# Row statistics by accumulating ScalarE passes in a two-part kernel, with another order of first banks, peaks and inputs

## What is computed

```
def _layernorm(x, eps=1e-05):
    m = jnp.mean(x, axis=-1, keepdims=True)
    v = jnp.var(x, axis=-1, keepdims=True)
    return (x - m) / jnp.sqrt(v + eps)

def mx_linear(x, W, b):            # blocks of 32 along the contraction, 8 bits, shared power of two
    return bf16_round(jnp.einsum('btk,ok->bto', mx_quant(x), mx_quant(W)) + b)

def _L0_ffn_ref(inputs, ln_w, ln_b, W1, b1, W2, b2):
    x = residual = bf16_round(inputs)
    h = mx_layernorm(x, ln_w, ln_b)          # mean and variance a second time
    h = mx_gelu(mx_linear(h, W1, b1))        # 1024 -> 4096
    h = mx_linear(h, W2, b2)                 # 4096 -> 1024
    return bf16_round(residual + h)

x = x + jnp.tanh(g_xattn[0]) * _L0_xattn_ref(ctx, ctx, _layernorm(x), ssm_kernel, D, 8)
x = x + jnp.tanh(g_ffn[0]) * _L0_ffn_ref(_layernorm(x), ln_w, ln_b, W1, b1, W2, b2)
```

## Time and profile before

| | |
|---|---|
| median of 3 runs | 1953.61 us (1953.2 to 1955.44) |
| profiled execution | 1954.59 us, its span 1952.8 us |
| PE busy | 1872.4 us, 96% |
| DVE busy | 1640.4 us, 84% |
| ACT busy | 1023.0 us, 52% |
| POOL busy | 881.6 us, 45% |
| mean granted TensorE clock | 0.987 |

### The profile page before, as it was taken

The page is one execution under the profiler, slowest core; times in us unless marked ns, Lnnn a source line. Parts: engine busy times, 40 slices in busy tenths (PEclk is TensorE's granted clock), DMA queues, the critical chain, the costliest instruction groups (busy, mean ns, idle before and its releaser), DMA issues. The chain is left out here.

```text
span 1952.8 us, 28581 instructions
## 1 busy us (share of the span) xinstructions
PE 1872.4 (96%) x11384; PEld 1473.2 (75%) x11432; DVE 1640.4 (84%) x1906; ACT 1023.0 (52%) x1271; POOL 881.6 (45%) x645
## 2 busy tenths in 40 slices
PE   6999999999999989998996997999999999999998
PEld 5888888888888879887885565666677766666773
DVE  5889999988888878888869898989888888889843
ACT  5565555555567767776723453444445544434440
POOL 3888889787888879997960000000000000000000
PEclk9999999999999999999998998999999999999999
DMA  7665657777666667776658421222122211221112
GB/s 243 207 217 170 182 173 223 241 243 256 222 207 186 226 202 230 227 229 207 200 202 300 138 73 53 65 76 77 44 76 77 76 66 55 66 76 55 44 44 76
DMA packets 165478, 294.24 MB, mean 151 GB/s; under 512 B 106145, under 2 KB 106145, under 8 KB 157153
## 3 DMA queue, kind: packets, MB, share of 16 engines
q1 hardware_dynamic: 165344, 292.41, 46.0%
HBM read 222.05 MB, written 45.68 MB: 137 GB/s over the span
## 5 line engine op out<-in xcount | busy, mean ns | idle before, releaser
L373 PE MATMUL y_ps<-kk_hi,slab 128*128 128x352 f32 (+6 forms) x3328 | 892.1, 352 | 33.0 <-DMA slab<-taps_scratch 18.3
L373 PEld LDWEIGHTS y_ps<-kk_hi,slab 128*128 128x128 f32 x3328 | 595.7, 189 | 103.2 <-issue 27.4
L373 PE MATMUL y_ps<-kk_lo,slab 128*128 128x512 f32 (+6 forms) x1664 | 582.0, 350 | 0.0
L1080 PE MATMUL l_ps<-f_xq_T,w_rest 128*128 128x256 bf16 x3136 | 349.2, 274 | 7.4 <-DMA f_xq_T<-f_hq 6.3
L1080 PEld LDWEIGHTS l_ps<-f_xq_T,w_rest 128*128 128x128 bf16 x3136 | 307.6, 98 | 47.6 <-issue 6.7
L373 PEld LDWEIGHTS y_ps<-kk_lo,slab 128*128 128x128 f32 x1664 | 315.1, 189 | 34.7
L861 POOL TENSOR_TENSOR terms<-terms 128x768 f32<-128x768 f32 x127 | 334.3, 2633 | 9.9
L1143 ACT ACTIVATE arena<-l_ps,b_c 128x256 bf16<-128x256 f32 x496 | 206.7, 472 | 248.7 <-PE l_ps L1080 243.4
L1381 POOL TENSOR_TENSOR f_rstd<-f_var_eps,f_neg_half 128x1 f32<-128x1 f32 x28 | 15.3, 548 | 673.0 <-DVE f_var_eps L1201 673.0
L1098 PE MATMUL acc_ps<-raw_room,arena 128*128 128x512 bf16 x993 | 224.6, 379 | 1.6
L1098 PE MATMUL acc_ps<-w_T,arena 128*128 128x512 bf16 x1007 | 222.9, 379 | 0.9
(11 more groups left out here) (148 smaller groups left out, 2295.3 us busy)
## 6 DMA issues: line engine op xcount, KB each, us to landing
slab<-taps_scratch SPq DMA_DIRECT2D x128, 512.0 KB, 4.9
arena<-in_w_m SPq DMA_DIRECT2D x32, 1024.0 KB, 6.8
arena<-x_scratch SPq DMA_DIRECT2D x60, 512.0 KB, 3.8
raw_room<-in_ctx_e SPq DMA_DIRECT2D x64, 384.0 KB, 3.3
arena<-in_w SPq DMA_DIRECT2D x22, 1024.0 KB, 7.5
x_tile<-in_x_t SPq DMA_DIRECT2D x32, 512.0 KB, 4.9
out_t<-arena SPq DMA_DIRECT2D x32, 512.0 KB, 2.6
w_scratch<-arena SPq DMA_DIRECT2D x22, 512.0 KB, 7.3
```

Source lines behind the costliest of these rows:

```text
L373: mm = nc.tensor.matmul(y_ps[:, y_base + begin:y_base + end], slab[s][:, half, d * P:(d + 1) * P], kk_part[s][:, begin - d * PAIR:end - d ...
L1080: mm = nc.tensor.matmul(l1_ps[bank % L1_BANKS][:, a, :], w1_tile(b)[:, k, a * P:(a + 1) * P], inputs[:, k, :], start=(k == 0), stop=(k == ...
```

## The change

Three things move.

1. The row statistics leave DVE. ACT makes them: an Identity pass with scale −1/L whose accumulator is the negated mean, a Square pass with that as its bias whose accumulator is the spread, and a small pass to variance + eps. The passes' main outputs are thrown away: the first pair writes into f_n, the second into the tile's loaded input (spent). SP's next load into that place waits for the second spread (sum2) in place of first_norm (n_ready).
2. first_banks takes bank 4 and 5 of both groups first, then two banks of group 0 to one of group 1, and the rest of group 1 at the end. DVE finishes weight tile 6 at once, and the peaks of group 0 stand behind tiles 8 and 12 (before: 6 and 11).
3. The inputs of groups 3 and 4 (tiles 6 to 9) move: ACT makes tile 4 between the last first banks, tile 5 between the gelus of group 1, tile 6 between banks 3 and 6 of group 2, tile 7 behind group 2's last gelu, and from then on both tiles of a group behind the gelu of a group. DVE weighs tiles 4 and 5 ahead of all peaks of group 1, and tile 7 behind three peaks of group 2. POOL takes each tile's two roots together while g < 4.

The diff, cut to its core:

```diff
-    for b in range(FILL, banks + LAG):
-        first_banks += [(0, b)] if b < banks else []
-        first_banks += [(1, b - LAG)] if b >= FILL + LAG else []
+    first_banks = [(g, b) for g in range(2) for b in range(FILL, KEPT)]
+    for b in range(KEPT, banks):
+        first_banks += [(0, b)]
+        first_banks += [(1, (b + KEPT) // 2)] if (b - KEPT) % 2 == 0 else []
+    first_banks += [(1, b) for b in range(banks) if b >= FILL and (1, b) not in first_banks]
...
-                    sp.wait_ge(n_ready, u - GROUP + 1)
+                    sp.wait_ge(sum2, u - GROUP + 1)
...
         def _(act):
+            def first_statistics(t):
+                i, u = t % GROUP, t - EARLY
+                x = xin[t % X_LOADS]
+                act.wait_ge(x1_loaded[u % X_LOADS], 16 * (u // X_LOADS + 1))
+                if u >= GROUP:
+                    act.wait_ge(hw_ready, u - GROUP + 1)
+                    act.wait_ge(rstd1, u - GROUP + 1)
+                nc.scalar.activation(n_bf[i][:], x, ACT.Identity, scale=-1.0 / L, accum_out=neg_mean1[i][:]).then_inc(mean1, 1)
+                act.wait_ge(mean1, u + 1)
+                if u >= 1:
+                    act.wait_ge(var1, u)
+                nc.scalar.activation(n_bf[i][:], x, ACT.Square, bias=neg_mean1[i][:], accum_out=spread1[:]).then_inc(sum1, 1)
+                act.wait_ge(sum1, u + 1)
+                nc.scalar.activation(var_eps1[i][:], spread1[:], ACT.Copy, scale=1.0 / L, bias=EPS).then_inc(var1, 1)
...
-                if b == banks - 1:
-                    if g == 1:
-                        gelu(1, 0)
-                        gelu(1, 1)
-                        gelu(1, 2)
-                    gelu(g, 3)
+                if (g, b) == (0, banks - 1):
+                    gelu(0, 3)
+                if (g, b) == (1, banks - 2):
+                    first_statistics(EARLY)
+            gelu(1, 0)
+            first_norm(EARLY)
+            gelu(1, 1)
+            second_statistics(EARLY)
+            first_statistics(EARLY + 1)
+            gelu(1, 2)
+            first_norm(EARLY + 1)
+            second_statistics(EARLY + 1)
+            gelu(1, 3)
...
-                        if g == 2 and b == 11:
-                            for s in range(GROUP):
-                                first_norm(GROUP * (g + 1) + s)
+                        if g == 2 and b == 3:
+                            first_statistics(GROUP * (g + 1))
+                        if g == 2 and b == 5:
+                            first_norm(GROUP * (g + 1))
+                        if g == 2 and b == 6:
+                            second_statistics(GROUP * (g + 1))
                     gelu(g, 3)
+                    if g == 2:
+                        first_statistics(GROUP * (g + 1) + 1)
+                        first_norm(GROUP * (g + 1) + 1)
+                        second_statistics(GROUP * (g + 1) + 1)
...
-                for s in range(GROUP):
-                    if g != 1 and g + 2 < groups:
-                        first_norm(GROUP * (g + 2) + s)
+                if g >= 2 and g + 2 < groups:
+                    for step in (first_statistics, first_norm, second_statistics):
+                        for s in range(GROUP):
+                            step(GROUP * (g + 2) + s)
...
         def _(dve):
-            def mean_var(src, out, stat_done, aggr_done, t):
-                nc.vector.bn_stats(stats[:, 0, :], src[:, 0:512])
-                nc.vector.bn_stats(stats[:, 1, :], src[:, 512:L]).then_inc(stat_done, 1)
...
                 weight_ints(j)
-                if j > KEPT:
+                if j > KEPT + 1:
                     weight_quant(j - 1)
                 weight_scales(j)
                 weight_clip(j)
-                if j in (KEPT, 11):
-                    peak(0, 0 if j == KEPT else 1)
+                if j == KEPT:
+                    weight_quant(j)
+                if j in (8, 12):
+                    peak(0, j // 4 - 2)
...
-                    if 1 <= g < groups:
+                    if 3 <= g < groups:
                         peak(g, s)
+                    if g == 2 and s == 0:
+                        for q in range(3):
+                            peak(g, q)
+                if g == 1:
+                    peak(g, 0)
+                    peak(g, 1)
```

More of the change, by code:

```diff
@@ L40 @@
 EARLY = 2 * GROUP
-LAG = 6
 W_TILES = 16
@@ L954, in ffn_block @@
         lnw_b, lnb_b = (sb(n, [P, L], F32) for n in ("lnw_b", "lnb_b"))
-        mv1 = [sb(f"f_mean_var1_{i}", [P, 2], F32) for i in range(GROUP)]
-        mv2 = [sb(f"f_mean_var2_{i}", [P, 2], F32) for i in range(GROUP)]
+        spread1, spread2 = sb("f_spread1", [P, 1], F32), sb("f_spread2", [P, 1], F32)
         neg_mean1 = [sb(f"f_neg_mean1_{i}", [P, 1], F32) for i in range(GROUP)]
@@ L1116, in _, with second_statistics @@
         def _(act):
+            def first_statistics(t):
[12 more added lines that the diff above has]
+                nc.scalar.activation(var_eps1[i][:], spread1[:], ACT.Copy, scale=1.0 / L, bias=EPS).then_inc(var1, 1)
+            def second_statistics(t):
+                i, u = t % GROUP, t - EARLY
+                spent = xin[t % X_LOADS]
+                act.wait_ge(n_ready, u + 1)
+                if u >= GROUP:
+                    act.wait_ge(rstd2, u - GROUP + 1)
+                nc.scalar.activation(spent, n_bf[i][:], ACT.Identity, scale=-1.0 / L, accum_out=neg_mean2[i][:]).then_inc(mean2, 1)
+                act.wait_ge(mean2, u + 1)
+                if u >= 1:
+                    act.wait_ge(var2, u)
+                nc.scalar.activation(spent, n_bf[i][:], ACT.Square, bias=neg_mean2[i][:], accum_out=spread2[:]).then_inc(sum2, 1)
+                act.wait_ge(sum2, u + 1)
+                nc.scalar.activation(var_eps2[i][:], spread2[:], ACT.Copy, scale=1.0 / L, bias=EPS).then_inc(var2, 1)
             def first_norm(t):
@@ L1213, in weigh_input @@
                     dve.wait_ge(const_loaded, 16 * 2)
-                if i == 1:
+                if i == 1 and t // GROUP == 3:
+                    dve.wait_ge(h_peak, 8)
+                elif i == 1 and t // GROUP > 3:
                     dve.wait_ge(mag1, 4 * (t // GROUP - 1) + 1)
@@ L1338, in _ @@
                 weight_clip(j)
-                if j in (KEPT, 11):
-                    peak(0, 0 if j == KEPT else 1)
+                if j == KEPT:
+                    weight_quant(j)
+                if j in (8, 12):
+                    peak(0, j // 4 - 2)
             weight_quant(W_TILES - 1)
             for g in range(groups + 2):
-                for s in range(GROUP):
-                    if 1 <= g and g + 1 < groups:
-                        second_statistics(GROUP * (g + 1) + s)
                 if g >= 2:
@@ L1364, in _ @@
                     hidden_quantise(g)
-                for s in range(GROUP):
-                    if g + 2 < groups:
-                        first_statistics(GROUP * (g + 2) + s)
                 if 2 <= g <= groups:
@@ L1393, in _ @@
             for g in range(2, groups):
-                for i in range(GROUP):
-                    first_rstd(GROUP * g + i)
-                for i in range(GROUP):
-                    second_rstd(GROUP * g + i)
+                if g < 4:
+                    for i in range(GROUP):
+                        first_rstd(GROUP * g + i)
+                        second_rstd(GROUP * g + i)
+                else:
+                    for i in range(GROUP):
+                        first_rstd(GROUP * g + i)
+                    for i in range(GROUP):
+                        second_rstd(GROUP * g + i)
 def gated_layer(nc, x_t, ctx_e, g_x, g_f, taps_in, skip_in, ln_w, ln_b, w1_t, w2_t, w_m, b1, b2, out_t):
```

28 lines of the change are left out of this document (4 added, 24 removed).

## The result

The changed kernel takes **1936.08 us** (median of 4 runs, 1934.2 to 1937.5), the kernel before 1953.66 us in the same comparison. The ratio is 0.9906 with a 95% interval of 0.9894 to 0.9918: 17.6 us less, where 1937.0 us had been forecast.

What follows compares the result with a forecast made beforehand. PE is full from 1224.34 us on; ahead of that it loses 44.5 us, following DVE's weight tiles and waiting for inputs and a bias. Losses of 28.2 instead gain 16.3 us: 1953.6 − 16.3 = 1937.3, rounded to 1937.0, range 1932 to 1942.

Steps and rivals of the forecast that it cites:

- Weights on DVE: First 24 banks: DVE's 3.0 us idle ahead of its first peak goes; PE loses 15.6 us instead of 22.4.
- Layer 2 of group 0 and group 2's input: PE waits 1.1 us for the quantised hidden rows, then 0.6 us for group 2's transposed input.
- Statistics: DVE sheds 1.69 us per tile and norm; ACT takes 2.56, its load growing to 35.3 us a group.
- Group 2's banks: POOL's tile 6 steps wait behind hidden_quantise(1), holding ACT; PE waits 2.4 us and loses 1.7 at low clock.
- POOL finds its gap: Rival for tile 6 in group 2: POOL gets through in time, PE's 4.1 us goes: 1933.4 us, chance 0.18.
- Group 3's banks: ACT's norm_again(3) waits for the reload; PE waits 5.1 us at the eighth bank, losing 1.7 at low clock.
- Later groups: From group 4 on ACT's block, 14 us or up to 27 with POOL's waits, fits; PE doesn't wait.
- the slower rival with passes twice as long: From group 4 on ACT's block takes 37.6 us; PE loses 7.3 us in 12 groups: 2025 us; slower: 0.04.
- DVE pays for POOL: Ahead of gated_sum(2), POOL's steps cost DVE 6.6 us: 1943.6 us; chance 0.13, shared with longer passes.
- Table loads and longer passes: Square outside gelu's table: some 15 us, 1952; passes a tenth longer: up to 1942, chance 0.13 shared with DVE paying.

Runs made afterwards that it cites:

- order_only: Kernel before with only the new first_banks order, tile 6 finished at once and group 0's peaks behind tiles 8 and 12; statistics stay on DVE: 1951.58 us.
- stat6_later: Changed kernel with tile 6's first statistics behind bank 4 of group 2 in place of bank 3: 1943.61 us.
- norm_later: Changed kernel with norm_again(3) behind bank 6 of group 3 in place of bank 2: 1928.14 us.
- triple_passes: Changed kernel with each of ACT's accumulating passes made three times for the tiles of groups 4 and up: 1987.81 us.
- double_passes: Changed kernel with each of ACT's accumulating passes made twice for the tiles of groups 4 and up: 1942.09 us.
- stat6_earlier: Changed kernel with tile 6's first statistics behind bank 1 of group 2 in place of bank 3: 1936.9 us.
- norm_later_again: Second run of the changed kernel with norm_again(3) behind bank 6 of group 3 in place of bank 2: 1929.18 us.

## Why the prediction was right, step by step

- **Weights on DVE: right.** DVE's first peak stands behind tile 8 without idle time, and the first banks lost 16.0 us (forecast 15.6). Of the 6.4 us that these banks lose less than before, order_only by itself keeps half: 3.2 us, DVE's idle time.
- **Layer 2 of group 0 and group 2's input: right.** 0.96 (forecast 1.1) and 0.48 (0.6). The moves of x_quant were counted on DVE's chain, and that chain was the bound.
- **Statistics: right in price.** A pass takes 1042 or 1149 ns and 187 ns more for reading the accumulator; a pair with its small pass takes 2.65 us (1120.74 to 1123.39), where the earlier trace rows gave 2.56. The Trainium skill ("ScalarE: Activation LUTs", Rules for kernel authors) prefers VectorE for additions and multiplications; by time alone that agrees (1.69 against 2.65 us), but DVE was the engine on the path.
- **Group 2's banks: right mechanism, term too large.** Forecast 2.4 + 1.7, measured 1.35 and 0.4 (1.7 together), with the granted clock at 1.00: the lower clock priced at 1.7 did not come behind so short a wait. The step that was off is the order of two events: the variance 0.4 us behind the start of hidden_quantise(1). In both profiles POOL's root was issued ahead of it, by 0.33 and 0.26 us; only the product was caught, until DVE's operation ended at 1128.23. That lies halfway to the rival "POOL finds its gap" (whose 3.6 us are not explained: its own words take off 4.1). A second step was off as well. The forecast had a caught root through behind the first of the three operations and the product behind the second; in stat6_later, and in ten groups of the changed kernel, the root ends with the second and the product with the third. PE's stretch is 7.8 us longer in stat6_later than in the changed kernel. So the 4.1 was too small for the order of events that it assumed, and the measured 1.7 came of that order being missed by a third of a microsecond.
- **Group 3's banks: right mechanism, size by two errors that cancel.** PE waits at the eighth bank, 4.35 us (forecast 5.1), released by the reload as said; norm_later shows that it is this one. But DVE's gated_sum(2) ends at 1177.96, which is 1179.2 on the forecast's clock (its network starts 1.22 later), 2.6 us ahead of the forecast 1181.8: DVE stood 0.37 us for tile 7, not 3.5. PE, which lost less in group 2, wanted the bank 1.8 us sooner too, so the wait came out 0.75 shorter. The lower clock behind it took 1.4 and 2.9 us in the two profiles (1.7 assumed).
- **Later groups: right that nothing waits; the reckoning behind it was not.** ACT's block behind a group was priced as passes plus POOL's whole wait. In the trace the second tile's first passes run while POOL waits, only one tile's steps meet the long operations (6.65 + 4.39 us, where 13.4 was reckoned), and some 15 us more fit in by triple_passes. ACT's load is 34.88 us a group (35.3 forecast). So the slower rival with passes twice as long (2025 us) could not have come; double_passes, which has that in groups 4 and up, takes 1942.1.
- **"DVE pays for POOL": did not come.** With POOL waiting behind many of them, DVE's operations (L1308, L1310, L1242, L1236) last 4426, 2294, 1284 and 1282 ns on the mean, 4425, 2293, 1284 and 1281 before. The Trainium skill ("Advanced Engine Details and Errata", VectorE Performance Modes) says that GpSimd instructions and Vector instructions on both ports block each other; every run here shows POOL's half only.
- **Table loads and longer passes: did not come.** ACT loads a table once in the network, as before (1.28 us at 1028.32). A pair of passes is 4% longer than the rows gave, not a tenth.

The sum of the terms was 28.2 us lost, the profiles show 25.0 and 26.5. So the terms gave 1.7 to 3.2 us less gain than the stretch shows. The forecast of 1937.0 lay 0.9 us above the median, nearer than its terms came to the stretch and within the spread that the start of the network gives: the path was right, the last microseconds are luck.

## What to carry to other kernels

Where a wait of the bound engine is taken away, the next thing to look for is the engine whose unbroken chain sets a later wait: here DVE's chain swallowed 1.7 us in stat6_earlier, until the wait behind it was moved as well, and 2.1 of 5.3 us in order_only. In an engine's fixed order a wait belongs behind the work that could still run (four biases ahead of norm_again were worth 5.4 to 7.3 us), before one tries to make the thing waited for faster. And small steps on a neighbour engine are to be priced with the long operations that they will meet, not at their own length.

## What the runs showed of the hardware that was not expected

- A step of POOL on one number a partition can last as long as the DVE operations in front of it: 0.55 us (root) and 0.19 (product) with none, 3.73 to 6.65 us behind one or two of 2.29 and 4.43. Each step got through at the end of a DVE operation, and the one behind it had to wait out the next: the root and the product of stat6_later ended 0.04 us behind operations that ended at 1132.21 and 1136.68. A root that began within the first of hidden_quantise's three operations took the end of two (in stat6_later, double_passes, triple_passes and the kernel after); one that began within the second, a root of triple_passes at 1288.19, was through at 1290.72, 0.41 us behind that operation's end and inside the third.
- Not every DVE operation holds POOL. In the kernel after, a root of 0.55 us at 1156.61 and a product of 0.19 at 1157.24 run inside a TENSOR_REDUCE (1155.65 to 1157.55), and the second tile's two steps at 1277.12 and 1277.74 take 0.54 and 0.19 inside an operation that reads PSUM (L1320, 1277.03 to 1278.25). Those that held it are a TENSOR_SCALAR of 16-bit numbers and TENSOR_TENSORs with both inputs in SBUF.
- The network's start moved by up to 5.9 us between executions of kernels with the same first part (1024.69 to 1030.55), about the spread between the runs of one kernel (1925.71 to 1933.48 us for norm_later_again, whose slowest run is the one that began at 1030.55).
- The same wait of PE costs different amounts at the lower clock behind it: 1.4 us behind 4.35 and 2.9 behind 4.13, in two executions of one kernel. Behind the wait of 1.35 in group 2 the granted clock stayed at 1.00.
